# Weight product ahead of the modulation, fp32r parts for two of its chunks, and weights loaded in turns, in an adaLN attention block

## The reference

```python
mod = (_silu(L0_c) @ L0_wmod).reshape(L0_c.shape[0], 6, 1, -1)
sa, ca, ga, sb, cb, gb = (mod[:, 0], mod[:, 1], mod[:, 2], mod[:, 3], mod[:, 4], mod[:, 5])
ga = (2 * (ga >= 0) - 1) * jnp.maximum(jnp.abs(ga), 0.25)
gb = (2 * (gb >= 0) - 1) * jnp.maximum(jnp.abs(gb), 0.25)
h = _layernorm(x, axis=-1) * (1 + ca) + sa
x = x + ga * _L0_attn_ref(h, L0_attn_Wq, L0_attn_Wk, L0_attn_Wv, L0_attn_Wo)
h = _layernorm(x, axis=-1) * (1 + cb) + sb
x = x + gb * _L0_ffn_ref(h, L0_ffn_factors, L0_ffn_bias)
```

## Time and profile before

| what | us |
|---|---|
| median of three runs | 476.99 |
| lowest and highest | 476.48, 477.9 |
| the profiled execution's own time | 480.09 |
| its span, first to last instruction | 477.9 |
| PE busy in the span | 454.9 |
| DVE, ACT, POOL busy | 364.6, 330.5, 243.8 |

### The profile page before, as it was taken

The page is one execution under the profiler, slowest core; times in us unless marked ns, Lnnn a source line. Parts: engine busy times, 40 slices in busy tenths (PEclk is TensorE's granted clock), DMA queues, the critical chain, the costliest instruction groups (busy, mean ns, idle before and its releaser), DMA issues.

```text
span 477.9 us, 7420 instructions
## 1 busy us (share of the span) xinstructions
PE 454.9 (95%) x2114; PEld 365.4 (76%) x2114; DVE 364.6 (76%) x630; ACT 330.5 (69%) x661; POOL 243.8 (51%) x315
## 2 busy tenths in 40 slices
PE   8999889987999999999999999999999979999995
PEld 3776667867888788888888788887888867777674
DVE  2896785877787779888786887877886578787765
ACT  2877745657777778787787777878887466567541
POOL 0476762441255565555555545455564474566454
PEclk9999999998999999999999999999999999999999
DMA  8968878754357736777878275878775236566502
GB/s 304 377 247 212 158 159 187 140 90 133 101 171 234 197 120 195 217 222 205 256 196 253 81 220 159 260 187 223 215 214 153 89 111 217 159 219 195 184 17 90
DMA packets 78199, 88.06 MB, mean 184 GB/s; under 512 B 4936, under 2 KB 55880, under 8 KB 78160
## 3 DMA queue, kind: packets, MB, share of 16 engines
q1 hardware_dynamic: 74208, 80.00, 55.3%
q0 software_dynamic: 3808, 7.34, 8.9%
q10 hardware_dynamic: 144, 0.26, 0.2%
HBM read 53.49 MB, written 34.10 MB: 183 GB/s over the span
## 4 chain that ended last, share of the span: by engine, by line
PE 32%; DVE 7%; DMA 7%; ACT 3%; POOL 3%; issue 2%; SPq 0%; DVEq 0%; POOLq 0%; ACTq 0%
PE ps_o L448 5%; PE ps_o L450 5%; PE ps_o L449 5%; DMA xb<-x_blocks 3%; DMA x_blocks<-xn 3%; PE ps_y L448 3%; PE ps_y L450 2%; PE ps_y L449 2%; PE ps_v L448 2%; PE ps_v L449 2%; PE ps_v L450 2%; ACT h_f L709 1%; PE ps_s L522 1%; PE ps_s L523 1%; POOL rstd L1322 1%
## 5 line engine op out<-in xcount | busy, mean ns | idle before, releaser
L1320 POOL TENSOR_SCALAR ve<-mv 128x1 f32<-128x1 f32 x64 | 21.4, 335 | 177.5 <-DVE mv L1070 125.4
L448 PE MATMUL ps_o<-v_lo,pt_hi 128*128 128x512 f32 x256 | 100.1, 391 | 1.8 <-DVE pt_lo L959 1.8
L450 PE MATMUL ps_o<-v_hi,pt_hi 128*128 128x512 f32 x256 | 99.7, 389 | 0.0
L449 PE MATMUL ps_o<-v_hi,pt_lo 128*128 128x512 f32 x256 | 99.6, 389 | 0.0
L959 DVE TENSOR_TENSOR h_lo<-h_f,h_hi 128x512 fp32r<-128x512 f32 (+1 forms) x67 | 50.0, 746 | 16.9 <-ACT h_hi L680 16.4
L448 PEld LDWEIGHTS ps_o<-v_lo,pt_hi 128*128 128x128 f32 x256 | 48.0, 188 | 13.9 <-issue 4.0
L450 PEld LDWEIGHTS ps_o<-v_hi,pt_hi 128*128 128x128 f32 x256 | 48.0, 188 | 10.1
L449 PEld LDWEIGHTS ps_o<-v_hi,pt_lo 128*128 128x128 f32 x256 | 48.1, 188 | 9.7
L709 ACT ACTIVATE h_f<-x1b,mod_t 128x128 f32<-128x128 f32 x120 | 53.0, 596 | 1.4 <-DVE x1b L1097 1.1
L448 PE MATMUL ps_y<-f_lo,h_hi 128*128 128x512 f32 (+1 forms) x124 | 48.5, 392 | 1.6 <-issue 0.9
L450 PE MATMUL ps_y<-f_hi,h_hi 128*128 128x512 f32 (+1 forms) x124 | 47.9, 386 | 0.0
(11 more groups left out here) (181 smaller groups left out, 1029.7 us busy)
## 6 DMA issues: line engine op xcount, KB each, us to landing
x_blocks<-xn SPq DMA_DIRECT2D x50, 256.0 KB, 2.6
p_blocks<-probs SPq DMA_DIRECT2D x24, 512.0 KB, 3.4
pb<-p_blocks SPq DMA_DIRECT2D x96, 128.0 KB, 3.2
x_ring<-in_x SPq DMA_DIRECT2D x16, 512.0 KB, 4.8
x1b<-x_blocks SPq DMA_DIRECT2D x30, 256.0 KB, 2.8
result<-x_ring SPq DMA_DIRECT2D x15, 512.0 KB, 3.0
f_sum<-in_factors POOLq DMA_DIRECT2D x14, 512.0 KB, 7.4
wmod<-in_wmod SPq DMA_DIRECT2D x12, 512.0 KB, 6.8
```

Of the source, the lines that this page charges most:

```text
L448: nc.tensor.matmul(acc, a_hi, b_lo, start=first, stop=False)
L449: nc.tensor.matmul(acc, a_lo, b_hi, start=False, stop=False)
L450: return nc.tensor.matmul(acc, a_hi, b_hi, start=False, stop=last)
L1320: nc.gpsimd.tensor_scalar(ve[:, one], mv[:, u, 1:2], EPS, None, ALU.add).then_inc(ve_done, 1)
```

## The change

The arithmetic stays the same up to rounding. What is done differently:

- **Loads.** Wv and Wo chunks 0 and 1 come first, each followed by its chunk of wmod's first third; x's first pair is loaded as two single tiles, the second one behind all of Wv and Wo; wmod's second third is issued ahead of x's pair 1.
- **PE.** Chunks 0 and 1 of Wvo are made ahead of and between SA and CA's chunks 0 and 1. In `project_weights` the hi-by-hi products of all four banks now come first, so that each third waits only for its own parts. SA and CA's chunks 2 and 3 are made of fp32r parts (`first_modulations`), with ACT making four more upper parts and DVE four more rests. The sum now lies in two groups of rows (0 to 3, and 32 to 35), and `first_columns` turns and adds both by a product with a 36 x 4 matrix of ones and zeros (`both_rows`), behind chunk 2 of Wvo.
- **Second third of wmod.** ACT makes all its upper parts in pair 0, chunks 0 and 1 with tile 0 and chunks 2 and 3 with tile 1. On POOL two inverse deviations move ahead. PE makes GA and SB in the middle of pair 1, between the values of tile 2 and the turning of tile 4.

```diff
             sp.dma_start(probs[:, early:early + C * B], c_t).then_inc(c_loaded, 16)
-            load_wmod(0)
-            load_v_and_o(0)
-            load_x(0)
-            for k in range(1, C):
+            for k in range(C // 2):
                 load_v_and_o(k)
+                load_wmod(0, [k])
+            sp.dma_start(x_ring[:, 0, :], x_pairs[0][:, 0, :]).then_inc(first_x_loaded, 16)
+            load_wmod(0, range(C // 2, C))
+            for k in range(C // 2, C):
+                load_v_and_o(k)
+            sp.dma_start(x_ring[:, 1, :], x_pairs[0][:, 1, :]).then_inc(x_loaded, 16)
             sp.dma_start(wqk_raw[:], wqk_t.rearrange("(c p) n -> p c n", p=P)).then_inc(wqk_loaded, 16)
+            load_wmod(1)
             load_x(1)
-            load_wmod(1)
...
+            def first_modulations(k):
+
+                if k < C // 2:
+                    pe.wait_ge(silu_steps, 4)
+                    pe.wait_ge(wmod_loaded[0][k], 16)
+                    for v in (SA, CA):
+                        nc.tensor.matmul(mod_banks[v][0:LO_ROW + B, :], silu_padded[:, k, :],
+                                         wmod_0[:, k, D * v:D * (v + 1)], start=(k == 0), stop=False)
+                else:
+                    pe.wait_ge(silu_steps, 7)
+                    pe.wait_ge(w_lo_done[0], 2 * (k - C // 2) + 2)
+                    for v in (SA, CA):
+                        for part in (m_lo, m_hi):
+                            last = nc.tensor.matmul(mod_banks[v][0:LO_ROW + B, :], silu_parts[:, k, :],
+                                                    part[:, 2 * k - C + v, :], start=False,
+                                                    stop=(k == C - 1 and part is m_hi))
                         if k == C - 1:
                             last.then_inc(mod_acc, 1)
+            def first_columns():
+                for v in (SA, CA):
+                    for k in range(C):
+                        at = (v * C + k) * B
+                        last = nc.tensor.matmul(mod_t_banks[0][:, at:at + B], early_rows[:, v, P * k:P * (k + 1)],
+                                                both_rows[:], start=True, stop=True)
+                last.then_inc(mod_tps, 1)
...
                 pe.wait_ge(weights_hi_done, 2 * k + 2)
-                pe.wait_ge(weights_lo_done, 2 * k + 2)
-                for m in range(C):
-                    last = three(wvo_banks[m][:], [part[:, k, P * m:P * (m + 1)] for part in wv_parts],
-                                 [part[:, k, :] for part in wo_parts], k == 0, k == C - 1)
-                    if k == C - 1:
-                        last.then_inc(wvo_acc, 1)
+                for i, (v, o) in enumerate(((0, 0), (1, 0), (0, 1))):
+                    if i:
+                        pe.wait_ge(weights_lo_done, 2 * k + i)
+                    for m in range(C):
...
-            pe.wait_ge(silu_steps, 3)
-            modulations((SA, CA))
-            project_weights(0)
+            for k in range(C // 2):
+                project_weights(k)
+                first_modulations(k)
             pe.wait_ge(ident_set, 2)
             transpose_x(0)
+            for k in range(C // 2, C):
+                first_modulations(k)
+            project_weights(2)
+            pe.wait_ge(both_rows_set, 3)
             pe.wait_ge(rows_done, 2)
-            modulation_columns(0, (SA, CA))
-            for k in range(1, C):
-                project_weights(k)
+            first_columns()
+            project_weights(3)
             pe.wait_ge(wqk_lo_done, 1)
             prep_pair(0)
-            modulations_by_parts((GA, SB))
-            with pe.Fori(1, PB - 1) as pair:
-                prep_pair(pair)
+            prep_pair(1, amid=lambda: modulations_by_parts((GA, SB)))
+            prep_pair(2)
...
             weight_parts(1)
+            first_modulation_parts(2)
             normalize_x(0, 0)
+            first_modulation_parts(3)
             weight_parts(2)
             weight_parts(3)
+            act.wait_ge(wqk_loaded, 16)
+            rounded(wqk_hi[:], wqk_raw[:]).then_inc(wqk_hi_done, 1)
             act.wait_ge(mod_t_done, 2)
             modulate_x(0, 0)
             normalize_x(1, 1)
-            act.wait_ge(wqk_loaded, 16)
-            rounded(wqk_hi[:], wqk_raw[:]).then_inc(wqk_hi_done, 1)
-            for k in range(C - 1):
-                first_wmod_parts(k)
             for m in range(C):
                 act.wait_ge(wvo_acc, m + 1)
                 rounded(wvo_hi[:, m, :], wvo_banks[m][:]).then_inc(wvo_hi_done, 1)
-            prep_pair(0, aside=lambda q: first_wmod_parts(C - 1) if q == 0 else None)
+            prep_pair(0, aside=lambda q: [first_wmod_parts(2 * q), first_wmod_parts(2 * q + 1)])
             act.wait_ge(w_lo_done[1], 2 * C)
...
             weight_rests(0)
+            weight_rests(1)
+            dve.wait_ge(first_x_loaded, 16)
+            x_stats(0, 0)
+            first_modulation_rests(2)
+            first_modulation_rests(3)
+            weight_rests(2)
             dve.wait_ge(x_loaded, 16)
-            x_stats(0, 0)
             x_stats(1, 1)
-            weight_rests(1)
-            row(SA)
-            row(CA)
+            first_rows()
+            weight_rests(3)
             columns(0)
-            weight_rests(2)
-            weight_rests(3)
...
+            of_x(2, 0)
             first_rests(0)
-            of_x(2, 0)
+            of_x(3, 1)
             first_rests(2)
             first_rests(3)
-            of_x(3, 1)
             of_x(4, 0)
             add_factor(1)
             pool.wait_ge(mod_acc, SB + 1)
```

More of the change, by code:

```diff
@@ L223, in adaln_block @@
         weights_hi_done, weights_lo_done = sem("weights_hi_done"), sem("weights_lo_done")
-        w_hi_done = [None, sem("w_hi_done1"), sem("w_hi_done2")]
-        w_lo_done = [None, sem("w_lo_done1"), sem("w_lo_done2")]
+        w_hi_done = [sem(f"w_hi_done{i}") for i in range(3)]
+        w_lo_done = [sem(f"w_lo_done{i}") for i in range(3)]
         mod_acc = sem("mod_acc")
@@ L310, in load_rows, with load_wmod @@
                 sp.dma_start(to[:, k, :], source[P * k:P * (k + 1), :]).then_inc(loaded[k], 16)
-            def load_wmod(i):
-                for k in range(C):
+            def load_wmod(i, chunks=range(C)):
+                for k in chunks:
                     load_rows(wmod_sb[i], wmod[:, 2 * D * i:2 * D * (i + 1)], k, wmod_loaded[i])
@@ L571, in prep_pair @@
                     project_values(2 * pair + u, u, prologue_v[u], 2)
+                    if u == 0 and amid is not None:
+                        amid()
             def scores_of(t):
@@ L928, in _, with second_gate_parts @@
                 wmod_parts(CB, k)
-            act.wait_ge(mod_acc, SB + 1)
+            def second_gate_parts(q):
+                act.wait_ge(mod_acc, SB + 1)
+                wmod_parts(GB, q - 2)
             with act.Fori(1, PB - 1) as pair:
-                prep_pair(pair, aside=lambda q: wmod_parts(GB, q - 2))
+                prep_pair(pair, aside=second_gate_parts)
             prep_pair(PB - 1, first_scores=True)
@@ L1260, in gate_of_result, with first_modulation_rests, first_rows @@
                 bound_gate(GB)
-            weight_rests(0)
+            def first_modulation_rests(k):
+                for v in (SA, CA):
+                    at = 2 * k - C + v
+                    dve.wait_ge(w_hi_done[0], at + 1)
+                    rest(m_lo[:, at, :], wmod_0[:, k, D * v:D * (v + 1)], m_hi[:, at, :]).then_inc(w_lo_done[0], 1)
+            def first_rows():
+                for v in (SA, CA):
+                    dve.wait_ge(mod_acc, v + 1)
+                    nc.vector.tensor_copy(early_rows[:, v, :], mod_banks[v][0:LO_ROW + B, :]).then_inc(rows_done, 1)
+                    rows[0] += 1
+            weight_rests(0)
+            weight_rests(1)
[4 more added lines that the diff above has]
+            weight_rests(2)
             dve.wait_ge(x_loaded, 16)
-            x_stats(0, 0)
             x_stats(1, 1)
-            weight_rests(1)
-            row(SA)
-            row(CA)
+            first_rows()
+            weight_rests(3)
             columns(0)
-            weight_rests(2)
-            weight_rests(3)
             dve.wait_ge(wqk_hi_done, 1)
```

58 lines of the change are left out of this document (34 added, 24 removed).

## The result

The changed kernel takes 487.95 us (median of 6 runs, 485.46 to 490.41), the kernel before in the same comparison 477.56 (476.48 to 481.71). The ratio is 1.0206, with a 95% interval of 1.0157 to 1.0254. A repetition (e14) gave 488.34 beside 480.41, ratio 1.0185 (1.0143 to 1.0226). The forecast was 481.4, range 478.6 to 484.0: right in sign, 6.5 us short. The profiled execution took 487.4 us, 7.3 us more than that of before; its span is 485.6 us.

What follows compares the result with a forecast made beforehand. PE was taken as the bound (454.9 of 477.9 us). Front -1.1, given back +1.2, pair 0 -0.5, rests +3.8, factor 0 +1.0 made +4.4 us on the median 476.99: 481.4, range 478.6 to 484.0.

Steps and rivals of the forecast that it cites:

- The front: PE's start, up to Wvo: done at 24.0 instead of 25.13, gain 1.1 us, given back (+1.2) by waiting for late columns.
- The rests: POOL's rests of wmod's second third end at 40.3; PE waits 2.3 us ahead of GA and SB: +3.8 us.
- pair 0: Tiles 0 and 1: the rest of h is quicker without POOL's rests beside it, q/k products at 29.4: gain 0.5 us.
- one rival: x's pair 1, landing 2 us later, delays Wvo's rests: about 483.1 us; chance 0.18 together with the clock rival.
- Factor 0: Its load waits for the eight rests and lands at 45.8; POOL waits before its first accumulating DMAs: +1.0 us.
- The landing: Factor 0's load by the skill's rule: an estimated 4.4 us for 1 MB, one less than the row; sum then 3.4.
- The level: The sum, +4.4 us, set against the median 476.99 instead of the profiled execution 480.09, which stands 3.1 over it.
- The rival with the clock at GA and SB: Clock falls too; GA, SB and the tile behind at half speed, 1.7 us more: 483.1; chance 0.18 with late load.

Runs made afterwards that it cites:

- e14: The changed kernel itself, unaltered, timed again beside the kernel before: 488.34 us beside 480.41, ratio 1.0185.
- e4: The changed kernel with factor 0 loaded into memory free at the time, without a wait for the eight rests: 484.65 us, ratio 1.0075.
- e17: The kernel before with one wait more on SP's list, so that factor 0 and the two x pairs behind it are issued late: 486.97 us, ratio 1.0157.
- e10: The changed kernel with the last factor's sum issued ahead of POOL's statistics of tile 7 instead of behind them: 486.93 us, ratio 1.0128.
- e7: The changed kernel with idle matmuls on PE in the prologue's two gaps and that of step 3: 486.52 us, ratio 1.0142.
- e16: The changed kernel with 9 warmup matmuls, and idle matmuls in step 3 and behind the transposes of step 24: 489.24 us, ratio 1.0168.
- e15: The changed kernel with 9 warmup matmuls instead of 7 and no other idle matmuls: 489.88 us, ratio 1.0194.

## Why the prediction was wrong

- **The front.** Half right. PE waited for tile 0's parts as forecast (1.29 us, forecast 1.2), because the columns were late. But the gain of 1.1 us on PE, which this wait was to eat, was not there. PE was to be done with Wvo at 24.0 and turned tile 1 at 25.23, though it began 0.4 us sooner than forecast: its work took 19.9 us and not 18.2 (the weight product 11.8 for 11.0, SA and CA 5.8 for 5.35, the columns 1.9 for 1.3, the turning 0.4 for 0.6). ACT modulated tile 0 at 22.77, not 21.7; tile 0's values came at 27.12, forecast 25.9. Of these 1.2 us 0.6 were left at GA and SB (41.01, forecast 40.4), where POOL's four rests took 5.00 us and not 5.67.
- **The rests.** Right: a wait of 2.27 us (forecast 2.3), tile 4 at 45.24 (44.7), 4.0 us later than before. The forecast for front, pair 0 and rests together was 3.4; e4, which has only them, is 3.3 us late at the first attention result. The later load of x's pair 1, which one rival reckoned with, cost nothing: DVE takes tile 2 at 25.38 without a wait for it.
- **Factor 0. This is the term of the sum that failed.** I set it at +1.0 us in all: one wait of POOL to 45.8, then 0.5 for the next half. From tile 4 (+4.0) to tile 6 (+6.2) the timeline has 2.2 us of it. e4 measures 2.4 to 2.8 us in the timeline and 5 to 6 us by the ratios, missing clock included. e17 measures 6.8 us at the first attention result without the late rests. That and the 3.3 of the rest are more than the 6.2 of both together, so the two losses run partly in parallel. The forecast for tile 5 was 50.8 and it came at 52.34; for tile 6 55.5, and 57.38. The sums are a chain of 14 accumulating DMAs, each waiting for the one before it on the same half; I followed the first link. It starts 7.5 us late, with the statistics of tiles 5 to 9 between its links on POOL's list. The sentence "from tile 7 on every engine is late by the same 4.4" should have been 6.2.
- **The landing.** The prediction cited the Trainium skill, "DMA: Bandwidth & Descriptors", section "Anatomy of one DMA — SWDGE (gpsimd) path", for 2.0 us plus bytes at 436 GB/s. By that rule a sum of 0.5 MB would land in an estimated 3.2 us. The trace disagrees: the 14 sums of the changed kernel, beside other loads, landed in 5.3 to 10.5 us, median 7.0. For a chain that waits for each landing this figure is the one that counts. Factor 0 itself, to which the prediction applied the rule, is no case for it: the section is on GpSimd's path, and SyncE loads factor 0. It landed in 5.5 us, near the 5.4 that the sum used.
- **Step 3.** Not in my sum. The gap there grew from 2.81 to 3.46 us, and the offset from 6.2 to 7.2; with the swap of e10 the wait is gone. It did not last: at the attention result ahead of the gap at 390 (381.30 before, 386.76 after) the offset is down to 5.5, for which I have no cause. One result later, behind the fall, it is 7.0.
- **The level and the clock. This is the larger part of the miss.** The sum on the timelines forecast 484.5 for the profiled execution, and that took 487.4: 2.9 short. The other 3.6 of the 6.5 us come from setting the sum against the median of three runs, 3.1 us under the profiled execution, as if the changed kernel would be free of what made that one longer. What the runs showed in its place: the profiled 480.09 was near the usual level (before's later medians are 480.4 to 481.3), and the changed kernel's median lies 0.6 us over its own profile. What moves the level is in good part the clock. The changed kernel has more and longer gaps and 2.7 to 3.9 us more missing clock than before. A fall costs 1.6 us where PE sets the pace and nothing where another chain does. From run to run of one kernel each us more of missing clock goes with about 0.85 us more time (241 runs of all kernels, each against the mean of its own; correlation 0.69). By that the extra missing clock is worth an estimated 2 to 3 us of the 8 to 10 lost; the idle matmuls of e7 gave back no more than that, and e16's less. How long a gap has to be for a fall stays open. The rival with the clock at GA and SB put the fall in a place where it costs nothing: there is none in the changed kernel's two profiles, and the one in e15 was covered.

## What to carry to other kernels

When a load is issued later, follow everything that waits in turn for it on an in-order queue, to the end of the chain, and not only its first wait: a chain of DMAs that each wait for the last moves as a whole and carries the short work queued between them. Two losses that meet at the same point are not simply added, and each is measured by putting it alone into the kernel before. Look at two profiles before you read a difference of 1 or 2 us off one: late loads, slow first products and a fall of the clock each made such a difference here. Before filling gaps for the clock, look whether the stretch behind the gap is bound by the engine whose clock it is: the same fall cost 1.6 us in one place and nothing in another.
